# DLRM tower, last layer: VectorE weighs both blocks of units, PE adds up the partitions with ones; two blocks reordered

## The chip, the cores and the metric

One core of a Trainium2 chip. The time is device microseconds of one execution, as the median of several runs. Engines work from their own in-order queues and wait for each other by semaphores: TensorE (PE), VectorE (DVE), ScalarE (ACT), GpSimd (POOL), and SyncE (SP), which here only issues transfers.

## The reference

For 2048 samples, 26 embedding rows of 128 numbers are looked up by index (`ids`) in 26 tables and joined with a dense row; all pairs of the 27 rows are multiplied (dot products), and the 351 results with the dense row go through three layers. All is float32.

```python
e = jnp.stack([tbl_0[ids[:, 0]], ..., tbl_25[ids[:, 25]]], axis=1)
combined = jnp.concatenate([e, r_dense_x[:, None, :]], axis=1)          # 2048 x 27 x 128
z = jnp.einsum('bfd,bgd->bfg', combined, combined)[:, _TRIU_I, _TRIU_J]  # 2048 x 351
h = jnp.concatenate([z, r_dense_x], axis=1)
h = jnp.maximum(h @ W_top1 + b_top1, 0.0)   # 479 -> 512
h = jnp.maximum(h @ W_top2 + b_top2, 0.0)   # 512 -> 256
y = h @ W_top3                              # 256 -> 1
```

## The kernel before

The samples are cut into 16 tiles of 128, four tiles to a block of 512 samples. In each tile, 18 embedding columns are gathered by GpSimd's indirect transfers (`gat`), 8 small tables are read with one-hot products on PE ("O" steps; VectorE builds the one-hot chunks into `ring`, eight per step), and PE transposes the gathered columns in five fills ("T", T0 to T4, two PSUM buffers), which ScalarE copies into `ct`. Then four gram chunks ("G0" to "G3", 8 groups each) make the pair products in PSUM; ScalarE and VectorE each copy two quadrants of every chunk into `z1`. When all four are copied, VectorE's `pick_pairs` transposes and compacts them into `zc`. In the next tile PE turns `zc` ("Z", three transposes into `back`) and ScalarE copies the result to `zt`. "P" is ScalarE's placing of the next tile's one-hot and dense columns (`place_columns`).

The three layers work on jobs: jobs 0, 1 and 2 are whole blocks of 512 samples, job 3 the first 256 samples of the last block, job 4 the 128 samples after those, and the tail job the last 128. A job has steps ("L", job, layer, m): four blocks of layer one, two of layer two, one last layer, seven in all, numbered 0 to 6 in the slices below. Units stand on partitions, samples on columns. ScalarE finishes each block (relu and bias into `h1` or `h2`, or the copy of the last layer's single row into `yrow`, which is row 0 of `h1`, from where SyncE stores it). All these steps share one PSUM bank `back`; for the last block the odd numbers of a layer use `prod` (`beside`). A step waits with `bank_clear` until the step before in its bank has been finished by ScalarE, and the first of a layer waits with `inputs_ready` for all the blocks of the layer below.

The order of PE's work is written out by hand in `tile_steps` (lines 76 to 110), and ScalarE's loop follows the same list. J stands for the steps of the block before, N for those of job 3, E for those of job 4. Jobs 0 and 1 have their last layer (J6) behind gram chunk G1 of tiles 7 and 11, job 2 between the first transposes of tile 14, job 3 (N6) between those of tile 15, and job 4 (E6) behind the last gram chunk of tile 15. VectorE's loop (lines 586 to 602) is written apart: pick_pairs of the tile before, the builds of one-hot chunks, then for each gram chunk its copy followed by two builds of the next tile's first one-hot step if it has one (tiles 12 to 15 have none), and pick_pairs(15) at the very end.

The last layer is, at lines 406 to 409, two matmuls with a single column of weights each, which add up in one PSUM row:

```python
for k in range(M2):
    ins = nc.tensor.matmul(dst[0:1, :], w3s[:, k:k + 1], h2[:, k, lo:hi],
                           start=(k == 0), stop=(k == M2 - 1))
```

Of the kernel before, what the change touches and what calls it, by code (L numbers as in the profile page):

```python
# [7 lines left out]
P = 128  # L8
# [9 lines left out]
NB = TILES // BT  # L18
# [57 lines left out]
def tile_steps(t):  # L76


    b, u = divmod(t, BT)
    last = b == NB - 1  # L80
    T = [("T", t, c) for c in range(TF)]
    G = [("G", t, c) for c in range(GC)]
    Z = [("Z", t - 1)]
    PL = [("P", t + 1)] if t + 1 < TILES else []
    O = [("O", b + 1, m) for m in range(NO)]

    def L(job):
        return [("L", job, 1, m) for m in range(M1)] + [("L", job, 2, m) for m in range(M2)] + [("L", job, 3, 0)]

    J = L(b - 1) if b else []  # L90
    N, E = L(NB - 1), L(NB)
    if t == 0:
        A = [("O", 0, m) for m in range(NO)]
        return (A[0:2] + T[0:1] + A[2:3] + T[1:2] + A[3:4] + T[2:3] + A[4:5] + T[3:4] + A[5:6] + T[4:5] + A[6:8]
                + [("P", 0)] + O[0:1] + G[0:1] + PL + G[1:])
    if t == TILES - 1:
        return T[0:1] + Z + T[1:2] + N[4:6] + T[2:3] + N[6:7] + E[0:2] + T[3:4] + E[2:4] + T[4:5] + G + E[4:]
    if last and u == 0:
        return T[0:2] + J[0:0] + T[2:4] + Z + T[4:5] + J[0:2] + G[0:1] + PL + G[1:2] + J[2:3] + G[2:4]
    if last and u == 1:  # L100
        return T[0:2] + J[3:4] + T[2:3] + Z + T[3:5] + J[4:5] + G[0:1] + PL + G[1:2] + J[5:6] + G[2:4]
    if last:
        return T[0:2] + J[6:7] + T[2:3] + Z + T[3:5] + N[0:2] + G[0:1] + PL + G[1:2] + N[2:4] + G[2:4]
    if u == 0:
        return T[0:2] + O[0:1] + T[2:4] + Z + T[4:5] + J[0:1] + G[0:1] + PL + G[1:2] + J[1:2] + G[2:4]
    if u == 1:
        return T[0:2] + O[1:2] + T[2:3] + J[2:3] + T[3:5] + J[3:4] + Z + O[2:3] + G[0:1] + PL + G[1:4]
    if u == 2:
        return T[0:2] + O[3:4] + T[2:3] + Z + T[3:4] + J[4:5] + T[4:5] + O[4:5] + G[0:1] + PL + G[1:2] + J[5:6] + G[2:4]
    return T[0:2] + O[5:6] + T[2:3] + Z + T[3:4] + O[6:7] + T[4:5] + O[7:8] + G[0:1] + PL + G[1:2] + J[6:7] + G[2:4]  # L110
# [27 lines left out]
def build(nc, dense_t, ids, ids_t, w1, b1, w2, b2, w3, out, tables):  # L138
    with ExitStack() as ctx:  # L139
        def sb(name, shape, dt=F32):  # L140
            return ctx.enter_context(nc.sbuf_tensor(name, shape, dt))
# [28 lines left out]
        b2s = sb("b2s", [P, M2])  # L170
        h1 = sb("h1", [P, M1, SB])
        h2 = sb("h2", [P, M2, SB])

        front = psum("front", [P, 2, TCH, P])
        prod = psum("prod", [P, SB])
# [14 lines left out]
        ident_ready = sem("ident_ready")  # L190
        rowid_ready = sem("rowid_ready")
        pads_ready = sem("pads_ready")
        hi_ready = sem("hi_ready")
        lo_ready = sem("lo_ready")
        transposed = sem("transposed")
# [132 lines left out]
        def _(pe):  # L328
# [45 lines left out]
            def inputs_ready(job, n):  # L374

                if n == 1:
                    b, _, hi = JOBS[job]
                    pe.wait_ge(back_free, BACK_INDEX[("Z", BT * b + hi // P - 1)] + 1)
                    return
                for m in range((M1, M2)[n - 2]):  # L380
                    step = ("L", job, n - 1, m)
                    if step in PROD_INDEX:
                        pe.wait_ge(prod_free, NO * NB + PROD_INDEX[step] + 1)
                    else:
                        pe.wait_ge(back_free, BACK_INDEX[step] + 1)
# [8 lines left out]
            def layer_block(bank, columns, n, m):  # L394
# [9 lines left out]
                    for k in range(M1):  # L404
                        ins = nc.tensor.matmul(dst, w2s[:, k, units], h1[:, k, lo:hi], start=(k == 0), stop=(k == M1 - 1))  # L405
                else:
                    for k in range(M2):
                        ins = nc.tensor.matmul(dst[0:1, :], w3s[:, k:k + 1], h2[:, k, lo:hi],  # L408
                                               start=(k == 0), stop=(k == M2 - 1))
                return ins  # L410

            pe.wait_ge(ident_ready, 1)
            for t in range(TILES):
                for kind, *q in tile_steps(t):
                    if kind == "T":
# [19 lines left out]
            pe.wait_ge(back_free, len(BACK_INDEX))  # L435
            pe.wait_ge(prod_free, NO * NB + len(PROD_INDEX))
            for i, (_, n, m) in enumerate(TAIL):
                if n > 1:

                    pe.wait_ge(tail_free, M1 if n == 2 else M1 + M2)  # L440
                layer_block(tail_banks[i], TAIL_JOB, n, m).then_inc(tail_done, 1)

        @block.scalar
# [96 lines left out]
        def _(dve):  # L540
# [14 lines left out]
            def copy_gram(t, c):  # L555
# [5 lines left out]
                                                gram[QUAD * j:QUAD * (j + 1), c % 2, :, NF * j:NF * (j + 1)])  # L561
                ins.then_inc(gram_dve, 1)

            def pick_pairs(t):
                dve.wait_ge(gram_act, GC * (t + 1))
                dve.wait_ge(gram_dve, GC * (t + 1))
# [5 lines left out]
                if t > 0:  # L572
# [3 lines left out]
                nc.vector.tensor_copy(zc[:, TOP * HALF:NPAIR].rearrange("p (g k) -> p g k", k=HALF),  # L576
                                      windows(z2, TOP, HALF)).then_inc(pairs_ready, 1)

            dve.wait_ge(rowid_made, 1)
            nc.vector.tensor_copy(rowid[:, :], rowid_i[:, :]).then_inc(rowid_ready, 1)  # L580
            dve.wait_ge(rowid_ready, 1)
# [4 lines left out]
            for t in range(TILES):  # L586
# [5 lines left out]
                else:  # L592
                    pick_pairs(t - 1)
                    for _, b, m in onehots_of(t)[1:]:
                        for k in range(OH_K):
                            build_chunk(b, m, k)
                for c in range(GC):
                    copy_gram(t, c)
                    for _, b, m in ahead:
                        for k in range(OH_K // GC * c, OH_K // GC * (c + 1)):  # L600
                            build_chunk(b, m, k)
            pick_pairs(TILES - 1)


def windows(z2, row, n):
# [34 lines left out]
```

## Time and profile before

| what | us |
|---|---|
| median of 3 runs | 437.32 (434.34 to 437.68) |
| the profiled execution | 433.56 |
| its span, first to last instruction | 431.4 |
| mean granted clock of PE | 0.984 |

The page gives busy time by engine, the clock that PE was granted in forty slices of the span, and the costliest groups of instructions by line. The timeline gives instructions in order of time; instructions of one line that follow each other are merged into one row (x their number). An entry in square brackets is the idle time of that engine just before, and what ended it. A float32 matmul appears as two records of weight load (PEld) and matmul (PE). A granted clock of 1.00 is 2.4 GHz, one of 0.50 is 1.2 GHz.

### The profile page before, as it was taken

What the parts mean: (1) busy time and instruction counts of PE and PEld (TensorE: products, weight loads), DVE (VectorE), ACT (ScalarE), POOL (GpSimd) and SP (SyncE); (2) the same over time, 40 slices, a digit from 0 to 9 for tenths busy, and PEclk for the clock granted to TensorE, in tenths of its full rate; (3) what the DMA queues carried; (4) which work ended last, traced back from release to release, by engine and by line L of the source; (5) the groups of instructions that cost most, each with busy time, mean ns of one, the idle gap of its engine ahead of it and who ended that gap; (6) DMA issues with size and microseconds to landing.
All of it is one profiled execution on the core that took longest, in us unless ns stands there. A gap on an engine that the chain in (4) does not pass through costs nothing. (4 is left out here: it accounts for less than half of the span.)

```text
span 431.4 us, 5888 instructions
## 1 busy us (share of the span) xinstructions
PE 377.1 (87%) x2184; PEld 300.8 (70%) x2184; DVE 209.0 (48%) x457; ACT 204.2 (47%) x339; POOL 298.3 (69%) x296
## 2 busy tenths in 40 slices
PE   0095788999999899999999899999998999997896
PEld 0074576988979686787778675877886566686785
DVE  0165795859594346192666265383654041413040
ACT  1105243656564555363546463554537355563432
POOL 5786787757787777777787777777787777775000
PEclk9998699999999999999999999999999999999899
DMA  6446395222222213222231213222211212221000
GB/s 156 161 153 186 103 239 160 57 79 74 74 92 74 79 51 97 79 74 74 63 102 52 80 49 97 81 75 72 55 44 50 56 51 54 55 52 48 2 0 2
DMA packets 19667, 34.53 MB, mean 80 GB/s; under 512 B 8427, under 2 KB 8942, under 8 KB 19640
## 3 DMA queue, kind: packets, MB, share of 16 engines
q0 software_dynamic: 9216, 18.89, 17.0%
q1 hardware_dynamic: 9904, 13.22, 10.4%
q10 hardware_dynamic: 520, 2.05, 1.3%
q8 instruction: 18, 0.29, 0.3%
q14 instruction: 9, 0.07, 0.0%
HBM read 34.13 MB, written 0.01 MB: 79 GB/s over the span
## 5 line engine op out<-in xcount | busy, mean ns | idle before, releaser
L308 POOL DMA_INDIRECT gat<-in_tbl,idx x288 | 296.3, 1029 | 97.2 <-issue 86.4
L347 PE MATMUL prod<-ring,tab_hi 125*128 125x512 f32 x256 | 106.2, 415 | 33.9 <-DVE ring L552 31.9
L560 DVE COPY z<-gram 32x216 f32<-32x216 f32 x128 | 49.2, 384 | 177.4 <-PE gram L364 175.4
L364 PEld LDWEIGHTS gram<-ct 128*128 128x128 f32 x1024 | 118.5, 192 | 10.2 <-issue 6.5
L364 PE MATMUL gram<-ct 128*128 128x108 f32 x1024 | 119.8, 275 | 1.5 <-ACT ct L472 0.7
L552 DVE TENSOR_SCALAR ring<-idb,rowid 125x512 fp32r<-125x512 int32 x256 | 110.1, 492 | 8.2 <-DMA idb<-in_ids_t 6.4
L349 PE MATMUL prod<-ring,tab_lo 125*128 125x512 f32 x256 | 103.1, 403 | 0.0
L347 PEld LDWEIGHTS prod<-ring,tab_hi 125*128 125x128 f32 x256 | 50.2, 196 | 46.9 <-issue 31.3
L472 ACT COPY ct<-front 128x512 f32<-128x512 f32 (+1 forms) x80 | 75.0, 1003 | 0.8 <-ACT h L500 0.4
L480 ACT COPY z<-gram 32x216 f32<-32x216 f32 x128 | 42.1, 329 | 53.3 <-PE gram L364 52.0
L349 PEld LDWEIGHTS prod<-ring,tab_lo 125*128 125x128 f32 x256 | 50.2, 196 | 9.8
L335 PE MATMUL front<-ident,gat 128*128 128x128 f32 x288 | 41.7, 273 | 4.5 <-ACT ct L472 4.5
L335 PEld LDWEIGHTS front<-ident,gat 128*128 128x128 f32 x288 | 33.8, 142 | 12.2 <-issue 9.6
L454 ACT COPY oh<-prod 128x512 f32<-128x512 f32 x20 | 11.7, 586 | 55.8 <-PE prod L349 55.8
L401 PE MATMUL back<-zt,w1z 117*128 117x512 f32 (+2 forms) x90 | 32.8, 500 | 0.0
L569 DVE STREAM_TRANSPOSE z<-z 128x864 f32<-128x864 f32 x16 | 31.0, 1937 | 0.5
L401 PEld LDWEIGHTS back<-zt,w1z 117*128 117x128 f32 x90 | 15.9, 190 | 14.7 <-issue 14.4
L464 ACT COPY ct<-oh 128x768 f32<-128x768 f32 x16 | 24.6, 1540 | 0.4
L405 PE MATMUL back<-h,w2s 128*128 128x512 f32 (+2 forms) x56 | 22.8, 554 | 1.7 <-ACT zt L487 1.5
L497 ACT ACTIVATE h<-back,b1s 128x512 f32<-128x512 f32 (+2 forms) x15 | 8.9, 595 | 27.9 <-PE back L401 27.9
L454 ACT COPY oh_last<-prod 128x512 f32<-128x512 f32 x12 | 7.0, 586 | 30.8 <-PE prod L349 30.8
L405 PEld LDWEIGHTS back<-h,w2s 128*128 128x128 f32 x56 | 10.4, 204 | 10.1 <-issue 7.2
(50 smaller groups left out, 157.6 us busy)
## 6 DMA issues: line engine op xcount, KB each, us to landing
idb<-in_ids_t SPq DMA_DIRECT2D x32, 256.0 KB, 3.3
gat<-in_tbl,idx POOLq DMA_INDIRECT x288, 2.6
oh<-in_dense_t SPq DMA_DIRECT2D x4, 256.0 KB, 3.5
oh<-in_tbl SPq DMA_DIRECT2D x2, 500.0 KB
w1z<-in_w SPq DMA_DIRECT2D x1, 702.0 KB
w2s<-in_w SPq DMA_DIRECT2D x1, 512.0 KB
gat<-in_tbl ACTq DMA_DIRECT2D x1, 500.0 KB
oh<-in_tbl ACTq DMA_DIRECT2D x1, 500.0 KB
```

What stands on the lines that cost most here:

```text
L308: nc.gpsimd.indirect_dma_start(out=gat[:, t % GS, i, :], out_offset=None, in_=tables[f][:, :], in_offset=bass.IndirectOffsetOnAxis(ap=idx[ ...
L335: ins = nc.tensor.transpose(front[:, (TF * t + c) % 2, n, :], gat[:, t % GS, col, :], ident[:, :])
L347: nc.tensor.matmul(prod[:, :], tab_hi[0:OH_P, m, k, :], ring[0:OH_P, k, :], start=(k == 0), stop=False)
L349: nc.tensor.matmul(prod[:, :], tab_lo[0:OH_P, m, k, :], ring[0:OH_P, k, :], start=False, stop=(k == OH_K - 1)).then_inc(used, 1)
L364: ins = nc.tensor.matmul(gram[:, c % 2, i, 0:SPG * NF].rearrange("p (j f) -> p j f", j=SPG), four.rearrange("p j f -> p (j f)"), four[:, : ...
L401: ins = nc.tensor.matmul(dst, w1z[0:ZP, k, units], zt[0:ZP, k, lo:hi], start=False, stop=(k == ZK - 1))
L405: ins = nc.tensor.matmul(dst, w2s[:, k, units], h1[:, k, lo:hi], start=(k == 0), stop=(k == M1 - 1))
L472: nc.scalar.copy(ct[:, t % 2, :, :, cols.start:cols.stop].rearrange("p g j f -> p f j g"), src).then_inc(front_free, 1)
L480: ins = nc.scalar.copy(z1[QUAD * j:QUAD * (j + 1), c * CG:(c + 1) * CG, :], gram[QUAD * j:QUAD * (j + 1), c % 2, :, NF * j:NF * (j + 1)])
L552: nc.vector.tensor_scalar(ring[0:OH_P, k, :], idb[0:OH_P, n % IDB, :], rowid[0:OH_P, k:k + 1], None, ALU.is_equal).then_inc(built, 1)
L560: ins = nc.vector.tensor_copy(z1[QUAD * j:QUAD * (j + 1), c * CG:(c + 1) * CG, :], gram[QUAD * j:QUAD * (j + 1), c % 2, :, NF * j:NF * (j ...
L569: nc.vector.transpose(z2[:, :, 0:QUAD], z1[:, :, :].rearrange("p g f -> p f g")).then_inc(z1_turned, 1)
```

## The change

The last layer no longer multiplies by the weights on PE. VectorE multiplies the first 128 units' block of `h2` by its weights (one number per partition), then multiplies the second block by its weights and adds the first, in place. PE adds up the 128 partitions with a column of ones in a single matmul. PE waits on a new semaphore `weighed` for it. VectorE does the weighing of jobs 0 to 3 between the copies of gram chunks 0 and 1 of the tile in which the last layer stands; job 4 is weighed behind tile 15's chunks and ahead of pick_pairs(15), and the tail job at the end. In tile 14, job 2's last layer moves from the transposes to behind G0, and the four blocks of job 3's layer one move by one slot each behind G1 and G2; in tile 15, job 3's last layer moves from the transposes to behind G1.

```diff
--- before.py
+++ after.py
@@ -94,13 +94,13 @@
         return (A[0:2] + T[0:1] + A[2:3] + T[1:2] + A[3:4] + T[2:3] + A[4:5] + T[3:4] + A[5:6] + T[4:5] + A[6:8]
                 + [("P", 0)] + O[0:1] + G[0:1] + PL + G[1:])
     if t == TILES - 1:
-        return T[0:1] + Z + T[1:2] + N[4:6] + T[2:3] + N[6:7] + E[0:2] + T[3:4] + E[2:4] + T[4:5] + G + E[4:]
+        return T[0:1] + Z + T[1:2] + N[4:6] + T[2:3] + E[0:2] + T[3:4] + E[2:4] + T[4:5] + G[0:2] + N[6:7] + G[2:4] + E[4:]
     if last and u == 0:
         return T[0:2] + J[0:0] + T[2:4] + Z + T[4:5] + J[0:2] + G[0:1] + PL + G[1:2] + J[2:3] + G[2:4]
     if last and u == 1:
         return T[0:2] + J[3:4] + T[2:3] + Z + T[3:5] + J[4:5] + G[0:1] + PL + G[1:2] + J[5:6] + G[2:4]
     if last:
-        return T[0:2] + J[6:7] + T[2:3] + Z + T[3:5] + N[0:2] + G[0:1] + PL + G[1:2] + N[2:4] + G[2:4]
+        return T[0:3] + Z + T[3:5] + G[0:1] + PL + J[6:7] + G[1:2] + N[0:2] + G[2:3] + N[2:4] + G[3:4]
     if u == 0:
         return T[0:2] + O[0:1] + T[2:4] + Z + T[4:5] + J[0:1] + G[0:1] + PL + G[1:2] + J[1:2] + G[2:4]
     if u == 1:
@@ -170,6 +170,7 @@
         b2s = sb("b2s", [P, M2])
         h1 = sb("h1", [P, M1, SB])
         h2 = sb("h2", [P, M2, SB])
+        ones = sb("ones", [P, 1])
 
         front = psum("front", [P, 2, TCH, P])
         prod = psum("prod", [P, SB])
@@ -190,6 +191,9 @@
         ident_ready = sem("ident_ready")
         rowid_ready = sem("rowid_ready")
         pads_ready = sem("pads_ready")
+        ones_ready = sem("ones_ready")
+        h2_scaled = sem("h2_scaled")
+        weighed = sem("weighed")
         hi_ready = sem("hi_ready")
         lo_ready = sem("lo_ready")
         transposed = sem("transposed")
@@ -377,7 +381,10 @@
                     b, _, hi = JOBS[job]
                     pe.wait_ge(back_free, BACK_INDEX[("Z", BT * b + hi // P - 1)] + 1)
                     return
-                for m in range((M1, M2)[n - 2]):
+                if n == 3:
+                    pe.wait_ge(weighed, job + 1)
+                    return
+                for m in range(M1):
                     step = ("L", job, n - 1, m)
                     if step in PROD_INDEX:
                         pe.wait_ge(prod_free, NO * NB + PROD_INDEX[step] + 1)
@@ -404,12 +411,11 @@
                     for k in range(M1):
                         ins = nc.tensor.matmul(dst, w2s[:, k, units], h1[:, k, lo:hi], start=(k == 0), stop=(k == M1 - 1))
                 else:
-                    for k in range(M2):
-                        ins = nc.tensor.matmul(dst[0:1, :], w3s[:, k:k + 1], h2[:, k, lo:hi],
-                                               start=(k == 0), stop=(k == M2 - 1))
+                    ins = nc.tensor.matmul(dst[0:1, :], ones[:, :], h2[:, 0, lo:hi], start=True, stop=True)
                 return ins
 
             pe.wait_ge(ident_ready, 1)
+            pe.wait_ge(ones_ready, 1)
             for t in range(TILES):
                 for kind, *q in tile_steps(t):
                     if kind == "T":
@@ -435,9 +441,11 @@
             pe.wait_ge(back_free, len(BACK_INDEX))
             pe.wait_ge(prod_free, NO * NB + len(PROD_INDEX))
             for i, (_, n, m) in enumerate(TAIL):
-                if n > 1:
-
-                    pe.wait_ge(tail_free, M1 if n == 2 else M1 + M2)
+                if n == 2:
+
+                    pe.wait_ge(tail_free, M1)
+                elif n == 3:
+                    pe.wait_ge(weighed, len(JOBS) + 1)
                 layer_block(tail_banks[i], TAIL_JOB, n, m).then_inc(tail_done, 1)
 
         @block.scalar
@@ -561,6 +569,22 @@
                                                 gram[QUAD * j:QUAD * (j + 1), c % 2, :, NF * j:NF * (j + 1)])
                 ins.then_inc(gram_dve, 1)
 
+            def second_layer_done(job):
+                for m in range(M2):
+                    step = ("L", job, 2, m)
+                    if step in PROD_INDEX:
+                        dve.wait_ge(prod_free, NO * NB + PROD_INDEX[step] + 1)
+                    else:
+                        dve.wait_ge(back_free, BACK_INDEX[step] + 1)
+
+            def weigh_units(job, columns):
+
+                _, lo, hi = columns
+                nc.vector.tensor_scalar(h2[:, 0, lo:hi], h2[:, 0, lo:hi], w3s[:, 0:1], None, ALU.mult).then_inc(h2_scaled, 1)
+                dve.wait_ge(h2_scaled, job + 1)
+                nc.vector.scalar_tensor_tensor(h2[:, 0, lo:hi], h2[:, 1, lo:hi], w3s[:, 1:2], h2[:, 0, lo:hi],
+                                               ALU.mult, ALU.add).then_inc(weighed, 1)
+
             def pick_pairs(t):
                 dve.wait_ge(gram_act, GC * (t + 1))
                 dve.wait_ge(gram_dve, GC * (t + 1))
@@ -576,6 +600,7 @@
                 nc.vector.tensor_copy(zc[:, TOP * HALF:NPAIR].rearrange("p (g k) -> p g k", k=HALF),
                                       windows(z2, TOP, HALF)).then_inc(pairs_ready, 1)
 
+            nc.vector.memset(ones[:, :], 1.0).then_inc(ones_ready, 1)
             dve.wait_ge(rowid_made, 1)
             nc.vector.tensor_copy(rowid[:, :], rowid_i[:, :]).then_inc(rowid_ready, 1)
             dve.wait_ge(rowid_ready, 1)
@@ -594,12 +619,23 @@
                     for _, b, m in onehots_of(t)[1:]:
                         for k in range(OH_K):
                             build_chunk(b, m, k)
+                third = [s for s in tile_steps(t) if s[0] == "L" and s[2] == 3 and s[1] < NB]
                 for c in range(GC):
+                    if c == 1:
+                        for _, job, _, _ in third:
+                            if job == 0:
+                                dve.wait_ge(weights_in, 16 * 6)
+                            second_layer_done(job)
+                            weigh_units(job, JOBS[job])
                     copy_gram(t, c)
                     for _, b, m in ahead:
                         for k in range(OH_K // GC * c, OH_K // GC * (c + 1)):
                             build_chunk(b, m, k)
+            second_layer_done(NB)
+            weigh_units(NB, JOBS[NB])
             pick_pairs(TILES - 1)
+            dve.wait_ge(tail_free, M1 + M2)
+            weigh_units(len(JOBS), TAIL_JOB)
 
 
 def windows(z2, row, n):
```

## Rows read from the trace of the kernel before

**Rows 1.** Page, engine totals: busy us (share of the span) and instructions.

```profile
PE 377.1 (87%) x2184; PEld 300.8 (70%) x2184; DVE 209.0 (48%) x457; ACT 204.2 (47%) x339; POOL 298.3 (69%) x296
```

**Rows 2.** Groups by line: shapes, count, busy us, mean ns, idle before, releasers.

```profile
L552 DVE TENSOR_SCALAR ring<-idb,rowid 125x512 fp32r<-125x512 int32 x256 | 110.1, 492 | 8.2 <-DMA idb<-in_ids_t 6.4 <-PE prod L349 0.4
...
L574 DVE COPY zc<-z 128x182 f32<-128x182 f32 x16 | 3.8, 238 | 0.0
L543 DVE TENSOR_TENSOR tab_lo<-oh,tab_hi 125x1024 fp32r<-125x1024 f32 x3 | 3.7, 1217 | 4.6 <-ACT tab_hi L447 4.6
```

**Rows 3.** Timeline of tile 7: start us, us, engine, line, operation, names, count.

```profile
227.81 0.78 DVE L560 COPY z<-gram 32x216 f32<-32x216 f32 x2 [4.89 <-PE gram L364]
...
228.62 0.91 DVE L552 TENSOR_SCALAR ring<-idb,rowid 125x512 fp32r<-125x512 int32 x2
...
229.49 1.88 PE L408 MATMUL back<-h,w3s 128*1 128x512 f32 x4
...
231.29 3.82 PE L364 MATMUL gram<-ct 128*128 128x108 f32 x32
```

**Rows 4.** Timelines of VectorE, then PE, in tile 11.

```profile
322.71 0.78 DVE L560 COPY z<-gram 32x216 f32<-32x216 f32 x2 [5.17 <-PE gram L364]
...
324.39 1.88 PE L408 MATMUL back<-h,w3s 128*1 128x512 f32 x4
```

**Rows 5.** Timelines of ScalarE, then PE in tile 14.

```profile
374.00 1.97 ACT L472 COPY ct<-front 128x512 f32<-128x512 f32 x2
...
374.07 1.88 PE L408 MATMUL back<-h,w3s 128*1 128x512 f32 x4
...
376.89 0.59 PE L391 MATMUL back<-ident,zc 128*117 128x128 f32 x3 [0.35 <-DVE zc L576]
...
378.46 0.67 PE L399 MATMUL back<-oh,w1d 128*128 128x256 f32 x2
```

**Rows 6.** Timeline of tile 15, T2 to the first gram chunk's copy.

```profile
402.66 0.60 PE L335 MATMUL front<-ident,gat 128*128 128x128 f32 x4
...
403.48 1.02 PE L408 MATMUL back<-h,w3s 128*1 128x256 f32 x4 [0.22 <-ACT h L497]
...
405.00 0.49 PE L399 MATMUL back<-oh,w1d 128*128 128x128 f32 x2 [0.50 <-ACTq L503]
...
410.21 7.39 PE L364 MATMUL gram<-ct 128*128 128x108 f32 x64 [0.71 <-ACT ct L472]
412.28 0.67 ACT L480 COPY z<-gram 32x216 f32<-32x216 f32 x2 [2.12 <-PE gram L364]
```

**Rows 7.** Timeline from the last gram copy to the end.

```profile
418.51 1.87 DVE L569 STREAM_TRANSPOSE z<-z 128x864 f32<-128x864 f32 x1
...
419.44 0.37 ACT L497 ACTIVATE h<-prod,b2s 128x128 f32<-128x128 f32 x1 [0.53 <-PE prod L405]
...
420.42 0.25 DVE L571 COPY z<-z 128x169 f32<-128x169 f32 x1
...
421.12 0.59 PE L391 MATMUL back<-ident,zc 128*117 128x128 f32 x3 [0.57 <-DVE zc L576]
421.74 0.48 ACT L487 COPY zt<-back 117x384 f32<-117x384 f32 x1 [0.90 <-PE back L391]
...
429.08 0.60 PE L408 MATMUL gram<-h,w3s 128*1 128x128 f32 x4 [0.46 <-ACT h L497]
```

**Rows 8.** Busy us by engine (x count) in stretches, PEclk, DMA, GB/s.

```profile
31.50:35.00 3.50, 1.33 (x9) 0.95 (x8) 1.95 (x4) 3.03 (x4) 0.85 (x1) 1.00 0.57 147
36.00:39.00 3.00, 3.00 (x8) 2.32 (x8) 2.58 (x5) 0.00 (x0) 2.39 (x3) 0.50 0.61 191
329.50:333.00 3.50, 2.17 (x19) 1.75 (x19) 2.81 (x4) 2.91 (x5) 2.59 (x4) 1.00 0.22 56
393.00:396.30 3.30, 0.22 (x3) 0.04 (x1) 3.07 (x6) 1.49 (x3) 2.69 (x3) 1.00 0.22 60
397.90:401.30 3.40, 3.40 (x9) 2.69 (x9) 0.00 (x0) 0.88 (x2) 0.00 (x0) 0.51 0.00 0
```

## Prediction

> **What bounds the kernel now.** I read the engine totals of the page first, then the groups by line, then the timeline of each place where a last-layer step stands, and last the clock by stretches. TensorE is busy 87% of the span, no other engine more than 69% [rows 1]; with tiles streaming through one in-order queue, a microsecond of PE work inside a tile is a microsecond of span unless PE has a wait there anyway. VectorE idles half the time, so the change looks like a free transfer of work. But its queue is in order too, and it sits inside the loop that releases PE: it copies each gram chunk out of PSUM and it ends every tile with pick_pairs, for which the turn of pairs ("Z") waits. Where tiles have no one-hot steps left to cover it, that wait shows: PE waits 0.35 us for zc at 376.89 and 0.57 at 421.12 [rows 5, 7]. After 418.51 the kernel is one chain: pick_pairs, turn, first layer, second layer, last layer, copy [rows 7]. Anything put ahead of pick_pairs(15) on VectorE is paid in full.
>
> **What goes.** A float32 matmul stands as two records, and the last layer of each of the six jobs as 4 (the x4 of L408 [rows 3 to 7]). The change leaves 2 each. Three jobs have 512 columns; in tile 7 the four records hold the queue from 229.49 to 231.29 (1.80 us) [rows 3], and they last the same 1.88 in tiles 11 and 14 [rows 4, 5]. So 0.90 us is saved per such job, 0.51 for job 3 (1.02 for 4 records [rows 6]) and 0.22 for the tail (4 records, about 0.11 apart, 0.60 in all [rows 7]).
>
> **What the two VectorE operations cost.** The multiply by one column of weights: L552 is a TENSOR_SCALAR of 512 columns at 0.49 us, L574 a copy of 182 at 0.24 [rows 2]; I take 0.49 for 512, on the line between them 0.30 for 256, and 0.24 for 128. The multiply-and-add with two tensors doesn't occur. The nearest is the two-tensor L543, 1024 columns at 1.22; the small end is L571, a copy of 169 columns at 0.25 [rows 2, 7]. The line between gives 0.64 for 512 and 0.35 for 256; for the second operand I add a little and take 0.67, 0.39 and, for 128, 0.28; bounds for 512 are 0.61 (half of L543) and 1.22. A start after a semaphore is about 0.04 after the release (the transpose starts at 418.51 and lasts 1.87, L571 starts at 420.42 [rows 7]). With three such gaps: 1.24 us for 512 columns (0.97 to 1.8), 0.81 for 256, 0.64 for 128.
>
> **Tile 7 (job 0).** VectorE weighs after it has copied chunk 0 and built two one-hot chunks; that work ends at 228.62 + 0.91 = 229.53 [rows 3]. Weighing ends at 230.77, and PE wanted the last layer at 229.49: a wait of 1.28, then 0.90 instead of 1.80. Net +0.38. VectorE's later copies and builds of this tile are behind by 1.2 us, but the next gram chunk takes PE 1.8, so they catch up.
>
> **Tile 11 (job 1).** No builds follow here. Chunk 0 is copied at 322.71 + 0.78 = 323.49; weighing ends 324.73, PE arrives at 324.39 [rows 4]: +0.34 - 0.90 = -0.56.
>
> **Tile 14 (job 2 and the reordering).** This is the largest term. Now the last layer of job 2 stands between transposes, 374.07 to 375.88, and what follows waits for zc until 376.89 anyway [rows 5]; zc hangs on the previous tile's chunks and not on this step. Taking the step out of there saves nothing. Put behind G0 it costs its whole length. Three parts: (a) Without job 3's first blocks between T4 and G0, G0 must wait for the ScalarE copies of T2 to T4. T0 and T1 are copied until 375.97 [rows 5]; T2's copy ends 376.97; the turn at 376.89 is copied from 377.51 (0.62 later, as 421.12 to 421.74 [rows 7]) until 377.99; T3 1.0 and T4 0.58 bring it to 379.55, G0 at 379.60. Before, PE went on with job 3 at 378.46 [rows 5]: +1.14. (b) G0 holds PE 1.78 us; its copies start 2.07 after its start (410.21 to 412.28 [rows 6]), VectorE's lasts 0.78, weighing 1.24, so the step may start 4.09 after G0 started. PE stands for 2.31. Nothing hides this: the blocks of job 3 are all queued behind. (c) The step itself, 0.90. Sum +4.35, at the bounds of the weighing +4.1 and +4.9. The rest of the tile is the same blocks and chunks, and pick_pairs(14) starts later by as much. The store of job 2 must land before ScalarE writes the first block of job 3 over its row; G1 and N0, over 3 us, cover that.
>
> **Tile 15 (job 3).** Before, its last layer took back at 403.48 and the next block waited for the copy and the release until 405.00, though T2 was queued out at 402.66 + 0.44 = 403.10 [rows 6]. With the step gone the blocks start at 403.10: -1.90. It comes back between G1 and G2: weighing ends 2.07 + 0.78 + 0.81 = 3.66 after G0's start and PE arrives after 3.57, so about 0.05 to 0.1 wait and 0.51 work. Net -1.35.
>
> **Ahead of pick_pairs(15) (job 4).** Weighing now stands before pick_pairs(15) and waits for ScalarE's second block of layer two, which ends at 419.44 + 0.37 = 419.81; before, the transpose started at 418.51 [rows 7]. It now starts at 419.81 + 0.64 + 0.02 = 420.46: +1.95, wholly on the chain. The saved records lie beside it and give nothing.
>
> **The tail.** From ScalarE's end to PE it was 0.04; now 0.64 for the two operations, minus 0.22 for two records: +0.37. The ones vector, its two waits and the semaphores lie in the start, where PE has nothing to do yet: 0.
>
> Sum without the clock: 0.38 - 0.56 + 4.35 - 1.35 + 1.95 + 0.37 = **+5.1 us**.
>
> **The clock.** PE's granted clock was 0.50 (1.2 instead of 2.4 GHz) after two stretches in which PE had mostly stood: 1.33 us busy of 3.5 just before 36.0, and 0.22 of 3.3 up to 396.3, where the low clock is seen from 397.9. It held after 2.17 of 3.5 [rows 8]. At 397.9 it stayed low for 3.4 us of full PE work, that is 1.7 us lost. The changed kernel makes two new idle stretches. Between 374.15 and 379.60 of tile 14 only T2, the turn, T3 and T4 run, some 2.0 us of 5.45, followed by G0 and the 2.31 wait. In the last stretch PE has one 0.4 us step between the end of layer two (419.4) and the turn (423.1). The second is as empty as those that were followed by 0.50, the first is close. I take one fall at each: 1.7 in tile 14 (0 to 3.4, since the wait behind G0 can prolong it) and 1.4 in the last stretch (1.0 to 1.7, part of the low time falling on short waits). Sum **+8.2 us**. The Trainium skill ("TensorE: Matmul & The Clock Gate", HAM oscillation) says that PE waits between bursts let the clock be gated again and that each one is paid anew; it is the rule that speaks against this change. By that rule the price would be two falls, and the trace agrees as far as 397.9 shows one.
>
> **How it stands to the median.** The sum is made against the profiled execution (433.56, span 431.4). The median shown is 437.32, 3.8 above it, so both kernels are forecast by the median: 437.32 + 8.2 = 445.5.
>
> **Rivals.**
> *Waits as above, clock holds.* For: the stretch of tile 14 isn't empty, and its share of work lies near that of 31.5 to 35.0 only by my reckoning of where T2 to T4 fall. The sum is +5.1: 442.4. Chance 0.22.
> *The two waits of tile 14 are shorter.* If T4's copy is out sooner or the weighing is at its low bound, and no fall follows: (a) 0 and (b) 2.04 give +2.9 instead of 4.35, and the sum 3.7; tiles 7 and 11 gain 0.27 each by the same bound: 3.2, so 440.5, within 1%. Against it: the ScalarE copies are back to back there. Chance 0.12.
> *The relief of PE decides.* If weighing were always ready when PE asks, the halves would be worth 3 x 0.90 + 0.51 + 2 x 0.22 = 3.65 and job 3's stall 1.90: 431.8, faster. That needs weighing to end before the gram chunk queued behind it has, also in tile 14, where the step is put directly behind the chunk whose copy precedes the weighing; the point where it turns is a wait under about 0.1 us there, the trace makes 2.3. Chance 0.05.
> The forecast with one or two falls has 0.61.
>
> About 1% (4.4 us) is what a measurement of this kernel can tell from no change. Faster than that: 0.05. Within: the third case and a little of the second, 0.13. Slower: 0.82. Range: from the short-wait case against the lower runs, 439.5, to two falls in tile 14 and the high bound of weighing, 449.5.
>
> **What the changed profile should show.** PE waits for weighed before the last layer: 1.3 us in tile 7, 0.3 in tile 11, 2.3 in tile 14; G0 of tile 14 over 1 us after T4; job 3's block without the stall on ScalarE's release; the transpose of pick_pairs(15) starting 0.6 to 0.7 after ScalarE's last layer-two block, and about 3 us after its gram copy; a clock of 0.50 inside tile 14 and after the last turn. I would be wrong if PE enters job 2's step without waiting, if zc in tile 14 comes earlier once the step is gone, or if the clock holds in both stretches.

## The result and the profile after

The changed kernel takes 446.86 us in the median of 6 runs (444.93 to 451.83); the kernel before takes 436.0 beside it (6 runs). The ratio is 1.0242 with a 95% interval of 1.0199 to 1.0286, so the change costs 10.5 us (8.7 to 12.5). Ratios and intervals here leave out executions more than 1.5% above the fastest of their kernel, while a median shown is of all, so that the two can differ by some tenths of a microsecond. The profiled execution has a span of 445.3 us against 431.4, a difference of 13.9: the profiled execution of before was faster than any of the six runs, and some 3 of the 13.9 are that.

Line numbers are of each kernel's own file; the gram matmuls are L364 before and L368 after.

The timeline of tile 7 in the changed kernel (start, duration, engine, line, operation), to be read against [rows 3]:

```profile
227.91 0.78 DVE L568 COPY z<-gram 32x216 f32<-32x216 f32 x2 [5.11 <-PE gram L368]
...
228.72 1.09 DVE L560 TENSOR_SCALAR ring<-idb,rowid 125x512 fp32r<-125x512 int32 x2
229.73 0.47 DVE L583 TENSOR_SCALAR h<-h,w3s 128x512 f32<-128x512 f32 x1
...
230.24 0.75 DVE L585 SCALAR_TENSOR_TENSOR h<-h,w3s 128x512 f32<-128x512 f32 x1
...
231.14 1.02 PE L414 MATMUL back<-h,ones 128*1 128x512 f32 x2 [1.49 <-DVE h L585]
232.09 1.14 PE L368 MATMUL gram<-ct 128*128 128x108 f32 x8
```

PE has nothing to do for 1.49 us until the weighing is done, and gram chunk G2 starts at 232.09 instead of 231.29, although the last layer itself is half as long.

Tile 14, the timeline of the same kernel, against [rows 5]:

```profile
375.71 0.63 PE L339 MATMUL front<-ident,gat 128*128 128x128 f32 x4 [1.05 <-ACT ct L480]
...
377.32 0.59 PE L398 MATMUL back<-ident,zc 128*117 128x128 f32 x3 [0.98 <-DVE zc L600]
...
377.74 0.82 PE L339 MATMUL front<-ident,gat 128*128 128x128 f32 x6
...
379.87 3.29 PE L368 MATMUL gram<-ct 128*128 128x108 f32 x16 [1.31 <-ACT ct L480]
...
383.19 0.78 DVE L568 COPY z<-gram 32x216 f32<-32x216 f32 x2 [5.93 <-PE gram L368]
...
384.01 0.48 DVE L583 TENSOR_SCALAR h<-h,w3s 128x512 f32<-128x512 f32 x1
384.53 0.75 DVE L585 SCALAR_TENSOR_TENSOR h<-h,w3s 128x512 f32<-128x512 f32 x1
...
385.42 1.86 PE L414 MATMUL back<-h,ones 128*1 128x512 f32 x2 [2.27 <-DVE h L585]
387.22 3.66 PE L368 MATMUL gram<-ct 128*128 128x108 f32 x16
```

The transposes now have gaps of 1.05 and 0.98 us between them, G0 waits 1.31 for the copies, and the last layer 2.27 for VectorE. Job 3's first two blocks, which stood between T4 and G0, now come behind G1, two chunks later, and cover the copies no longer. And everything from G0 on is slow: one gram chunk of 16 records takes 3.29 and 3.66 us, where [rows 6] has 64 records in 7.39. The stretches of the same kernel (busy us of PE first, the granted clock third from the end), against [rows 8]:

```profile
374.20:379.80 5.60, 2.33 (x18) 1.64 (x15) 2.92 (x6) 5.04 (x7) 4.38 (x5) 1.00 0.20 54
380.50:390.50 10.00, 7.73 (x30) 5.79 (x30) 2.00 (x4) 3.40 (x5) 7.68 (x8) 0.50 0.21 54
427.90:431.60 3.70, 0.39 (x3) 0.13 (x3) 3.05 (x6) 0.62 (x2) 0.00 (x0) 1.00 0.00 0
432.00:438.00 6.00, 5.43 (x25) 5.12 (x25) 0.00 (x0) 1.22 (x3) 0.00 (x0) 0.50 0.01 3
```

PE worked for 2.33 of 5.6 us and then ran at 1.2 GHz for 10 us; it worked for 0.39 of 3.7 and then ran at 1.2 GHz for over 6. The Trainium skill ("TensorE: Matmul & The Clock Gate", HAM oscillation) says that waits of PE between bursts bring back the half clock, each anew; the trace agrees, with two such places that before didn't have. Not every wait is followed by it: behind the 1.49 us of tile 7 the clock is 1.00 from 228 to 240.

The end of the changed kernel, against [rows 7]:

```profile
427.94 0.37 ACT L505 ACTIVATE h<-prod,b2s 128x128 f32<-128x128 f32 x1 [0.53 <-PE prod L412]
428.41 0.29 DVE L583 TENSOR_SCALAR h<-h,w3s 128x128 f32<-128x128 f32 x1 [1.50 <-ACT h L505]
428.73 0.35 DVE L585 SCALAR_TENSOR_TENSOR h<-h,w3s 128x128 f32<-128x128 f32 x1
429.00 1.85 DVE L593 STREAM_TRANSPOSE z<-z 128x864 f32<-128x864 f32 x1
429.23 0.38 PE L414 MATMUL back<-h,ones 128*1 128x128 f32 x2 [1.33 <-DVE h L585]
...
431.59 0.99 PE L398 MATMUL back<-ident,zc 128*117 128x128 f32 x3 [1.98 <-DVE zc L600]
...
443.17 0.38 PE L414 MATMUL gram<-h,ones 128*1 128x128 f32 x2 [1.17 <-DVE h L585]
```

The transpose of pick_pairs(15) waits for ScalarE's last block of job 4 (ends 428.31) and for the weighing. From the last turn to the last step it takes 11.58 us (431.59 to 443.17) where it took 7.96 (421.12 to 429.08 [rows 7]).

### The profile page after: what moved, and what is told of

Same layout as the page of the kernel before. It is cut to its first block and busy times, and to the rows that moved or that the text cites. A ratio compares the mean times of both kernels' runs of the same rounds, so it can differ in the third digit from the quotient of the medians.

```text
span 445.3 us, 5882 instructions
## 1 busy us (share of the span) xinstructions
PE 380.9 (86%) x2172; PEld 306.1 (69%) x2172; DVE 214.5 (48%) x470; ACT 204.1 (46%) x339; POOL 302.0 (68%) x296
## 3 DMA queue, kind: packets, MB, share of 16 engines
q1 hardware_dynamic: 9904, 13.22, 10.3%
## 5 line engine op out<-in xcount | busy, mean ns | idle before, releaser
L312 POOL DMA_INDIRECT gat<-in_tbl,idx x288 | 299.9, 1041 | 96.3 <-issue 86.5
L368 PEld LDWEIGHTS gram<-ct 128*128 128x128 f32 x1024 | 121.5, 196 | 14.0 <-issue 7.8
L368 PE MATMUL gram<-ct 128*128 128x108 f32 x1024 | 123.4, 280 | 2.8 <-ACT ct L480 2.0
```

The lines of the kernel that those rows point to most:

```text
L312: nc.gpsimd.indirect_dma_start(out=gat[:, t % GS, i, :], out_offset=None, in_=tables[f][:, :], in_offset=bass.IndirectOffsetOnAxis(ap=idx[ ...
L368: ins = nc.tensor.matmul(gram[:, c % 2, i, 0:SPG * NF].rearrange("p (j f) -> p j f", j=SPG), four.rearrange("p j f -> p (j f)"), four[:, : ...
```

## The experiments

Beside some of the runs the kernel before itself took 629.5 or 637.4 us instead of 436. Those runs are marked "630 us", their ratios stand beside a before of their own, and I read their traces only in stretches that look like those of the 436 us runs. The changed kernel itself has no 630 us run. No kernel leaves out part of the computation; the filling matmuls add work whose results nobody reads. The edits are shown shortened.

**The clock alone.** In the changed kernel, the waits of PE are filled:

```diff
+ def fill(bank, n):
+     for _ in range(n): nc.tensor.matmul(bank, w1d[:, 0:P], w1d[:, :], start=True, stop=True)
+ # tile 14: 1 ahead of the turn, 1 ahead of G0, 2 ahead of job 2's last layer
+ # end: 1 ahead of job 4's last layer, 2 ahead of the last turn
```

> The changed kernel, with idle matmuls added where PE waits, nothing else: their results are never read, and they come out of w1d into banks that are free at that point. One of 512 columns (0.86 us) ahead of the turn in tile 14, one between T4 and G0, two ahead of job 2's last layer, one ahead of job 4's, two ahead of the last turn. Theory A (the waits cost 5 to 6 us, and the low clock that follows them costs the other 4 to 6): the clock stays at 1.00 through tile 14 and through the last stretch, and the time is 4 to 6 us shorter than the changed kernel's 446.9, so 4.5 to 6.5 above before. Rival B (the low clock only accompanies the waits, all of the loss is the waits): no gain, or up to 1 us longer from the added work: 10 to 11 above before.

> The changed kernel with idle matmuls where PE waits, as r1_filled (results never read; one of 512 columns, 0.86 us, ahead of the turn in tile 14, one between T4 and G0, two ahead of job 2's last layer, one ahead of job 4's, two ahead of the last turn), again, since in the call with r1_filled the kernel before itself took 629.5 us and PE stood waiting for its own instructions. Where before takes about 436: Theory A (waits cost 5 to 6 us, the low clock that follows them 4 to 6 more): 4.5 to 6.5 us above before, clock 1.00 through tile 14 and the last stretch. Rival B (all of the loss is the waits): 10 to 11 above.

r1_filled, 630 us: ratio 1.0101 (1.0056 to 1.0147), 6.4 us above its before, inside the 4.5 to 6.5 of theory A. s1_filled: 440.7 us against 435.46, ratio 1.0129 (1.0090 to 1.0169), 5.6 us above before. The change costs 4.9 us less with seven matmuls more; from the two intervals I estimate 2.4 to 7.4 for this difference. Stretches of s1_filled:

```profile
381.00:391.00 10.00, 9.16 (x50) 6.73 (x51) 2.95 (x6) 4.63 (x9) 7.56 (x9) 1.00 0.21 54
424.00:428.00 4.00, 3.45 (x12) 1.12 (x10) 3.07 (x6) 0.62 (x2) 0.00 (x0) 1.00 0.00 0
428.00:434.00 6.00, 4.97 (x40) 4.59 (x41) 0.00 (x0) 1.95 (x5) 0.00 (x0) 1.00 0.01 3
```

The clock stays at 1.00 in both places, while VectorE's late work is unchanged. So about half of the loss is the low clock, and the other half, 5.6 us, is the waits and the exposed step. Theory A holds; rival B, a loss of waits alone, falls. The traces say the same by place: tile 14, from its first transposes to those of tile 15, takes 24.19 us (374.74 to 398.93) instead of 27.59, and the last turn to the last step 8.66 (427.94 to 436.60) instead of 11.58, 6.3 us less in the two.

**The order of tile 14.** In the changed kernel, the old order comes back, and job 2 is weighed in tile 13:

```diff
-        return T[0:3] + Z + T[3:5] + G[0:1] + PL + J[6:7] + G[1:2] + N[0:2] + G[2:3] + N[2:4] + G[3:4]
+        return T[0:2] + J[6:7] + T[2:3] + Z + T[3:5] + N[0:2] + G[0:1] + PL + G[1:2] + N[2:4] + G[2:4]
@@ VectorE, ahead of the copy of chunk 3
+                    if (t, c) == (TILES - 3, 3):
+                        second_layer_done(2)
+                        weigh_units(2, JOBS[2])
```

> The changed kernel with the order of tile 14 as it was before; job 2 is weighed in tile 13, between the copies of chunks 2 and 3, so that its last layer can stand among the transposes of tile 14 again. Theory A (the move of job 2's last layer exposes it and its wait, 4.4 us, and lets the clock fall in tile 14, 2 to 4): 6 to 8 us shorter than the changed kernel, 3 to 5 above before; tile 14 takes within 0.5 us of what it took before. Rival B (the cost lies in VectorE's weighing as such and in the last stretch, the order is worth under 2 us): 8.5 to 10 above before.

> As r2_order14_back (the changed kernel with tile 14's order as before, job 2 weighed in tile 13), again for the same reason. Theory A (the move of job 2's last layer exposes it, its wait and a low clock): 3 to 5 us above before. Rival B (the order is worth under 2 us; VectorE's weighing and the last stretch carry the loss): 8.5 to 10 above before.

r2_order14_back, 630 us: 1.0080 (1.0046 to 1.0114). s2_order14_back: 439.39 us, ratio 1.0098 (1.0065 to 1.0132), 4.3 us above before, 6.2 less than the change. From the start of tile 14's transposes to that of tile 15's it takes 19.96 us (374.53 to 394.49), against 27.59 in the changed kernel (373.62 to 401.21) and 19.48 in before (373.10 to 392.58). Theory A holds: the order of one tile, with the wait for VectorE and the low clock that come with it, carries more than half of the loss. This run takes back both the order and the wait; r6 and s6 below part them.

The same reordering in the kernel before, with two matmuls on PE and nothing on VectorE:

> The kernel before with only the order of tile 14 changed: job 2's last layer, still two matmuls of PE with nothing of VectorE, stands behind G0, and job 3's blocks stand where the change puts them. Theory A (of the 4.35 forecast for this tile 1.14 is G0 waiting for the copies of T2 to T4 and the rest the exposed step): 1.0 + 1.8 = 2.8 us above before, up to 4.5 if the clock falls between the transposes. Rival B (the order costs nothing by itself, only together with the wait for VectorE): within 1 us of before.

> As r4_order14_alone (the kernel before with only tile 14's order changed, nothing of VectorE). Theory A (G0 waits 1.0 us for the copies of T2 to T4, and the step of 1.8 us is exposed): 2.8 above before, up to 4.5 where the clock falls between the transposes. Rival B (the order costs nothing by itself): within 1 us.

Both are 630 us runs: ratios 1.0054 (1.0004 to 1.0104) and 1.0082 (1.0039 to 1.0125), 3.4 us (0.3 to 6.5) and 5.2 (2.5 to 8.0). The order costs something without VectorE; how much where before takes 436 us wasn't measured. The timeline of s4_order14_alone shows how:

```profile
578.30 1.49 PE L335 MATMUL front<-ident,gat 128*128 128x128 f32 x6
580.89 3.75 PE L364 MATMUL gram<-ct 128*128 128x108 f32 x16 [1.10 <-ACT ct L472]
584.57 1.95 PE L408 MATMUL back<-h,w3s 128*1 128x512 f32 x4
586.44 2.04 PE L364 MATMUL gram<-ct 128*128 128x108 f32 x16
```

G0 waits 1.10 us for ScalarE's copies and the step stands exposed between two chunks. The 3.75 us of its G0 are at a clock of 0.50 that was there before tile 14 (0.50 from 570 to 575 as well), so this trace doesn't show whether the order alone makes the clock fall; s6_weigh_before_g0 below does.

**Job 4 back on PE.** In the changed kernel, nothing stands ahead of pick_pairs(15):

```diff
-            second_layer_done(NB)
-            weigh_units(NB, JOBS[NB])
             pick_pairs(TILES - 1)
@@ layer_block: job 4 takes the two matmuls with w3s as before
```

> The changed kernel, but job 4's last layer is made by PE with its two matmuls as before, so that VectorE goes from the last gram copy straight into pick_pairs(15). All else as changed. Theory A (the transpose of pick_pairs starts 2.0 us earlier, and PE's waits in the last stretch are again too short for the clock to fall, worth 1.4 to 2.9): 3.4 to 5 us shorter than the changed kernel, 5.5 to 7 above before, with the clock at 1.00 from 415 to the end. Rival B (waits only): 2.0 shorter, clock low in the last stretch all the same.

> As r3_job4_on_pe (the changed kernel, but job 4's last layer made by PE's two matmuls, so that pick_pairs(15) follows the last gram copy at once). Theory A (the transpose starts 2.0 us earlier and PE's waits in the last stretch are too short for the clock to fall there, worth 1.4 to 2.9): 5.5 to 7 us above before, clock 1.00 from the last gram chunk to the end. Rival B (waits only): 8 to 8.5 above, clock low in the last stretch as in the changed kernel.

Both are 630 us runs: 1.0125 (1.0074 to 1.0176) and 1.0148 (1.0094 to 1.0201), 7.9 and 9.4 us above their before. Neither is in the 5.5 to 7 that theory A gave, and they can't be set against the 10.5 us, so the times decide nothing. But the end of the kernel is the same there as elsewhere, and can be read. The timeline of s3_job4_on_pe (PE alone):

```profile
626.58 1.07 PE L414 MATMUL back<-h,w2s 128*128 128x128 f32 x8
627.49 1.06 PE L414 MATMUL prod<-h,w2s 128*128 128x128 f32 x8
629.09 0.60 PE L420 MATMUL back<-h,w3s 128*1 128x128 f32 x4 [0.55 <-ACT h L512]
630.26 0.58 PE L400 MATMUL back<-ident,zc 128*117 128x128 f32 x3 [0.57 <-DVE zc L607]
...
638.92 0.38 PE L418 MATMUL gram<-h,ones 128*1 128x128 f32 x2 [1.17 <-DVE h L592]
```

and the stretches:

```profile
632.00:636.00 4.00, 3.54 (x32) 3.35 (x31) 0.00 (x0) 1.47 (x4) 0.00 (x0) 1.00 0.02 4
```

From job 4's second layer to the last step it takes 12.34 us (626.58 to 638.92); in the changed kernel it takes 17.24 (425.93 to 443.17), 4.9 more: 2.0 for the later transpose and 2.9 for the low clock behind it, which here stays at 1.00. In that stretch theory A's price is shown; the whole kernel's time at a before of 436 is not. In before the same stretch took 11.64 (417.44 to 429.08); the 0.70 between them is the weighing of the tail.

**Where VectorE weighs.** In the changed kernel, one edit:

```diff
                 for c in range(GC):
-                    if c == 1:
+                    if c == 0:
                         for _, job, _, _ in third:
```

> The changed kernel with one edit: jobs 0 to 3 are weighed ahead of the copy of gram chunk 0 of the same tile instead of behind it, where VectorE stands idle for 5 us and more. PE's order stays as changed. Theory A (PE waits because the weighing is queued behind the chunk copy): the waits of 1.5, 0.5, 2.3 and 0.3 us in tiles 7, 11, 14 and 15 are gone, and with the one in tile 14 the second stretch of low clock: 5 to 7.5 shorter than the changed kernel, 3 to 5.5 above before. Rival B (the wait is set by the length of the two operations or their own semaphores, not by their place): 0 to 2 shorter.

> As r6_weigh_before_g0 (the changed kernel with jobs 0 to 3 weighed ahead of the copy of gram chunk 0 instead of behind it), again where the kernel before takes about 436. Theory A (PE waits because the weighing is queued behind the chunk copy): no wait for VectorE before the last layers of jobs 0 to 3, 3 to 5.5 us above before. Rival B (the wait is set by the two operations themselves): 8 to 10 above.

r6_weigh_before_g0, 630 us: 1.0162 (1.0100 to 1.0224), 10.3 us. s6_weigh_before_g0: 444.83 us against 436.23, ratio 1.0207 (1.0156 to 1.0259), 9.0 us above before. The expectation of 3 to 5.5 failed. Half of its mechanism is there: the last layers of jobs 0 to 3 follow their chunk without a wait, as in tile 14, the last three rows of its PE timeline here. The other half is not: it had the low clock of tile 14 gone with the wait. The first two rows are from tile 12, and the rows by themselves are the stretches behind them and from G0 of tile 14 on:

```profile
331.05 0.66 PE L339 MATMUL front<-ident,gat 128*128 128x128 f32 x4 [1.19 <-DMA gat<-in_tbl,idx]
336.02 1.11 PE L339 MATMUL front<-ident,gat 128*128 128x128 f32 x4 [4.32 <-DMA gat<-in_tbl,idx]
...
386.17 3.75 PE L368 MATMUL gram<-ct 128*128 128x108 f32 x16 [1.31 <-ACT ct L480]
389.85 1.86 PE L414 MATMUL back<-h,ones 128*1 128x512 f32 x2
391.64 2.38 PE L368 MATMUL gram<-ct 128*128 128x108 f32 x16
```

```profile
336.00:344.00 8.00, 7.18 (x15) 3.96 (x16) 0.00 (x0) 1.92 (x3) 6.17 (x7) 0.50 0.21 55
386.00:392.00 6.00, 5.83 (x20) 3.94 (x20) 0.77 (x2) 2.12 (x5) 4.61 (x5) 0.50 0.22 55
```

Tile 14 takes 24.51 us (379.84 to 404.35) instead of 27.59: the wait for VectorE was worth 3.1. But it is still 5.0 above the 19.48 of before, with nobody waiting for VectorE. G0, the step and G1 hold PE for 3.68, 1.79 and 2.22 us at a clock of 0.50 up to 392, where at 1.00 they hold it for 1.78, 0.95 and 1.78: 3.2 us of low clock. The other 1.8 are the step and G0's wait for the copies. So what brings the low clock is the thinly filled stretch of transposes ahead of G0, 1.87 us of work from 381.0 to 386.0, and not the wait for VectorE behind it. The changed kernel's own trace agrees: its clock falls at 380.4, inside G0 and before that wait.

From tile 1 to tile 12 this kernel gains what its halved steps promise: that way takes 1.7 us less than in before, for two steps of 0.90. Then in tile 12 PE waits for gathered rows, 6.3 us in all, and the clock is 0.50 behind that: from tile 12 to 13 it takes 30.44 us instead of 22.67. The gain of the earlier tiles is lost at another bound. The profiled execution (449.26) was the slowest of its runs, and its last gather starts later (403.37) than in the other five 436 us traces, so how the missing 4 us divide between tile 12 and tile 14 in a median run stays open; the two intervals, of the change and of this kernel, overlap.

**A mixed kernel.** Jobs 0, 1 and 3 weighed ahead of chunk 0 and summed by ones, jobs 2, 4 and the tail as before, tile 14 ordered as before, tile 15 as changed; and the same with three filling matmuls between T0 and the turn of tile 15:

```diff
+ WEIGHED = [0, 1, 3]
+ # s9_mixed_filled only, ahead of turn_pairs(14):
+     pe.wait_ge(prod_free, NO * NB + PROD_INDEX[("L", NB - 1, 1, 3)] + 1)
+     fill(prod[:, :], 3)
```

> Put together from what the terms say: the last layers of jobs 0, 1 and 3 weighed by VectorE ahead of gram chunk 0 and summed by ones, jobs 2, 4 and the tail on PE as before; tile 14's order as before, tile 15's as changed. Theory A (the halved step is a gain where VectorE had idle time before PE asks: 0.9 + 0.9 in tiles 7 and 11, 1.3 from job 3's step that no longer stalls tile 15): 2.5 to 3.5 us below before. Rival B (work taken from PE is worth nothing, since a tile waits for copies and zc anyway): within 1 us of before.

> r7_mixed (the last layers of jobs 0, 1 and 3 weighed by VectorE ahead of gram chunk 0, jobs 2, 4 and the tail on PE, tile 14's order as before and tile 15's as changed), and besides three idle matmuls of 512 columns (2.6 us, results never read) in the 3.1 us in which PE waits for zc between T0 and the turn of tile 15. Theory A (halved steps are a gain where VectorE is early, 3.1 us, and the low clock behind that wait, 1.7 us, goes with the wait's emptiness): 4 to 5.5 us below before, clock 1.00 from 50 us to the end. Rival B (work taken off PE is worth nothing and the clock falls anyhow): within 1.5 us of before.

r7_mixed, 630 us: 0.9989 (0.9947 to 1.0030), no difference. s9_mixed_filled: 434.2 us against 436.23, ratio 0.9941 (0.9898 to 0.9983), 2.6 us faster than before (0.7 to 4.4), the only kernel that beats it. By the medians of all runs it is 2.0. That is half of what was expected, and its interval doesn't shut out rival B's 1.5. Of its trace, a row of PE's timeline in tile 12, and three stretches:

```profile
332.91 1.12 PE L341 MATMUL front<-ident,gat 128*128 128x128 f32 x4 [1.90 <-DMA gat<-in_tbl,idx]
```

```profile
333.00:339.00 6.00, 5.37 (x13) 3.18 (x14) 0.00 (x0) 1.92 (x3) 4.60 (x5) 0.50 0.22 57
394.00:398.70 4.70, 4.19 (x22) 2.41 (x20) 3.47 (x7) 1.79 (x4) 3.73 (x4) 1.00 0.21 56
398.70:430.00 31.30, 26.95 (x206) 24.04 (x206) 6.44 (x14) 13.05 (x31) 1.94 (x3) 1.00 0.03 7
```

The filled wait of tile 15 keeps the clock at 1.00 to the end, where before has 0.51 for 3.4 us [rows 8]. But PE came to tile 12 at 328.29 instead of 329.85, waited 1.90 us for gathered rows, and the clock fell there. In this trace each term of theory A is there in its size: 1.7 us from tile 1 to tile 12 (forecast 0.9 + 0.9), and from tile 15's first transposes to job 4's second layer 21.88 us (394.98 to 416.86) instead of 24.86, 3.0 less (forecast 1.3 + 1.7). But tile 12 takes 26.61 us instead of 22.67 and spends 3.9 of it: more than was saved in tiles 7 and 11.

## Why the prediction was right

The forecast was slower by 8.2 us, 445.5 in 439.5 to 449.5; measured are 446.86 and +10.5 (8.7 to 12.5). Sign and mechanism stand, the sum was short by 2.3. That 445.5 lies within 1.4 of the measured median is partly luck: it starts from the 437.32 of three runs, and six runs of before gave 436.0. Step by step, from the profiled pair, which lies 13.9 apart and not 10.5, so that the rows add up to about 3 us more than the change costs:

| step | forecast, us | measured, us | how it is read |
|---|---|---|---|
| tile 7 | +0.38 | +0.70 | G2 0.80 late, 0.10 of it before the tile |
| tile 11 | -0.56 | -0.30 | 0.81 late before, 0.51 behind |
| tile 14, waits, step and low clock | +6.05 | +8.1 | T0 to T0, 27.59 against 19.48 |
| tile 15 up to job 4's second layer | -1.35 | -0.14 | 8.63 late before, 8.49 behind |
| weighing ahead of pick_pairs(15) | +1.95 | +1.98 | last turn 10.47 late |
| low clock in the last stretch | +1.4 | +2.9 | ScalarE's last block 13.38 late |
| tail | +0.37 | +0.49 | last copy 13.87 late |

**Right.** Each wait stands where it was put: 1.49, 0.48, 2.27 us before the last layers of tiles 7, 11, 14 (forecast 1.28, 0.34, 2.31), 1.31 before G0, and the transpose 0.69 behind ScalarE's block. The stall that job 3 made in tile 15 is gone as forecast: from T2 to the next block it is 0.44 us (412.30 to 412.74) instead of 2.34 [rows 6]. The waits and the step alone were summed to 5.1, and s1_filled, which takes the low clock of the two new places away, measures 5.6 (3.9 to 7.3). One agreement is luck: 2.27 against 2.31 in tile 14 was forecast for the full clock. There the wait would be 2.5 by the late weighing; the low clock made G0 hold PE 1.5 us longer and its copies start only 1.25 later, which took the difference back.

**The terms that were mis-sized.** The term that was too small is the price of the low clock. It was taken at 1.7 + 1.4 = 3.1 us; the difference between the change and s1_filled is 4.9, and the trace of the change has 3.8 + 2.9. In tile 14 the price of a fall was read from 397.9 to 401.3 [rows 8], where PE's work was dense and the clock came back. Here the low clock made G0's copies come 3.32 us after its start instead of 2.07, the weighing behind them later, and PE then stood 2.27 us at the low clock, which stayed low until 390.5: G0's copies +1.25, the step +0.85, G1 +1.7, 3.8 in all. The upper bound named for it, 3.4, was nearly right, and the text had its reason ("the wait behind G0 can prolong it"); the value taken was not. The reason was also only a small part of it: s6_weigh_before_g0, without that wait, still has 3.2 us of low clock in tile 14. In the last stretch the low clock covered three of the four first-layer blocks of the tail, 2.9 us and not 1.4. A further 1.0 us is in tile 15: the turn to T2 takes 7.42 us (404.88 to 412.30) instead of 6.40 (396.26 to 402.66), since the same fall came sooner against the work (0.5 us ahead of the turn, where before has it 1.4 behind) and lasted over 6 us instead of 3.4 [rows 8]. The forecast took it as unchanged. Whether this 1.0 belongs to the change isn't shown: with the same order of tile 15, s1_filled, s2_order14_back and s6_weigh_before_g0 have 6.04, 6.34 and 6.40 there, and s3_job4_on_pe, a 630 us run, has 7.37.

Small sizes: the two-tensor operation was taken at 0.67 and takes 0.75 for 512 columns, PE starts 0.14 to 0.15 behind it and not 0.04, and the halved step holds PE for 0.95 and not 0.90; with the builds of tile 7, which end a little later, that is the 0.3 missing in each of tiles 7 and 11. Two slips of the working: 0.49, 0.67 and three gaps of 0.04 are 1.28 and not 1.24, and the low bound of 0.97 for the weighing lies under its two operations alone (0.49 + 0.61 = 1.10), so the rival of the shorter waits was put about 0.8 us too low. The Trainium skill ("VectorE: DVE Perf Modes", the part on the TRN2 errata) has a two-tensor addition in float32 of 512 columns at 691 ns; this one, with a multiplication by a number per partition, takes 751 in the mean of three.

**Of the rivals,** "clock holds" (+5.1) is what s1_filled measures, so it was a true alternative; with PE's waits filled, the clock holds. "The relief of PE decides" found no support in the change. In s6_weigh_before_g0 and s9_mixed_filled, without waits for VectorE, the relief is the sum of the halved steps up to tile 12 (1.7 us for 1.8) and is lost there to gathered rows: I had counted PE as the only bound up to tile 14, and in these two traces it was the only one up to tile 12.

## What to carry to other kernels

Before work is moved to an idle engine, ask what stands behind it in that engine's queue and what work stood in the gap that it leaves: a step that filled a wait costs nothing where it is and its full length elsewhere. Count a stretch in which TensorE mostly waits twice, once as itself and once as the low clock that can follow it, and count the second by what the slow stretch makes late in turn. Taking away the wait behind such a stretch doesn't bring the clock back. A gap that can't be closed can be filled: seven idle matmuls took 4.9 us off this kernel.

## What the runs showed that I had not expected

**GpSimd is a second bound.** The totals give it 69% [rows 1], but its timeline is gathers 0.94 us long, 0.30 apart: 1.25 us each, 18 per tile. In before its last longer rest is 4.03 us at 90.07, for PE's transposes; from there to its last gather at 395.38 it has none. That is 22.5 us a tile, where PE takes 23.5 in the mean of tiles 3 to 11. In before, counting the gathers, the fourth fill of tile 12 was issued by 326.4 and transposed at 332.85; in s6_weigh_before_g0 it was issued by 334.4 and PE stood for it until 336.02. For before, the groups by line call 86.4 us of the gaps "issue". Single gathers take 2 to 5 us (3.66 at 219.38 in before, 4.05 at 218.87 in the changed kernel, 5.24 at 125.00 in s6_weigh_before_g0). They stand at nearly the same times in all six 436 us traces, at 125 to 128, at 219 to 222 and at 313 to 317, but their lengths differ from one to the next (2.07 to 5.24 us at the second); why isn't shown. Where they add up to a late gather and PE is early, tile 12 waits. A busy share is not the share of time in which an engine is free to take more.

**Runs in which the same kernel takes 1.45 times as long.** In the 630 us runs PE stands without a reason that the trace names. The groups by line of r4_order14_alone begin

```profile
L308 POOL DMA_INDIRECT gat<-in_tbl,idx x288 | 284.1, 986 | 281.0 <-PE front L335 191.0 <-issue 83.3 <-DMA idx<-in_ids 6.6
L364 PE MATMUL gram<-ct 128*128 128x108 f32 x1024 | 148.5, 303 | 93.3 <-issue 59.3 <-DVE z L560 28.0 <-ACT z L480 4.1
```

PE's gram matmuls stand 59 us with no releaser in the trace, often 1.0 us ahead of a single one, and the gathers wait 191 us for PE's transposes, where before has 4.6 in its 436 us trace; the mean granted clock is 0.83. What starves PE there isn't shown by the trace and wasn't tried. It isn't shown to be the chip either: chip 3 stands on record beside a before of 629.5 and beside one of 435.46. A ratio from such a run says little about a term of the other.
